# The last 64 features in two token halves: matmuls of 64 weight columns instead of zero-padded ones of 128

## The chip, the cores and the metric

The kernel runs as one program on one core of a Trainium2 chip. The metric is the device time of that core in microseconds (us). Three runs of the kernel before are shown, and one more execution was profiled.

## The reference, cut to what matters

32 images become 38 tokens of 192 features each, in float32. Two layers follow. The first has a state-space scan whose four step inputs come from small networks, and a mixture of eight feed-forward experts of which each token uses two. The second has a mamba block that is run in both directions of the sequence, and a mixture of eight 192 by 192 experts:

```python
h = h + _L0_attn_ref(_layernorm(h), ...)   # scan, 16 states per feature
h = h + _L0_ffn_ref(_layernorm(h), ...)    # 2 of 8 experts, 768 wide
h = h + _L1_attn_ref(_layernorm(h), ...)   # down to 96, mamba forward and backward, up to 192
h = h + _L1_ffn_ref(_layernorm(h), ...)    # sum over e of gate[e] * (x @ expert_w[e].T + expert_b[e])
```

In the mamba block `z` and `x` are projections of 96 values to 192, the convolution over four taps and the step width `dt` (24 to 192) give 192 features as well, and `y = (h * C).sum(-1)` sums 16 states for each of the 192 features.

## The kernel before

**Layout.** Features lie on partitions, tokens along the free axis. The images are worked on in four groups of eight, T = 304 tokens a group. 192 features don't fit on 128 partitions, so each result has a main part, features 0 to 127 for 304 tokens, and a rest, features 128 to 191. In the packed layout the rest of tokens 0 to 151 lies on partitions 0 to 63 and that of tokens 152 to 303 on partitions 64 to 127, in 152 further columns (T to PK = 456). VectorE, ScalarE and GpSimd so handle 456 columns of 128 partitions.

**How the rest is computed before.** Every matmul of the kernel has weights of more than 64 columns, most of exactly 128. For a packed rest two of them accumulate into the same 128 partitions: the first with the rest's 64 weight columns followed by 64 columns of zeros, on the first token half, the second with 64 zero columns followed by the weights, on the second half. The weights lie in memory as main, zeros, rest, zeros (with_blanks, line 2222), and halves (line 159) cuts the three windows of 128 columns out of it. This is done for the z projection (project_z), the four convolution taps (project_taps), the step width (packed), delta (to_delta) and, with a matrix of ones (gsumr), for the sum over states (add_states). A float32 matmul shows in the trace as two weight loads and two matmul instructions.

The expert mixture's rest isn't packed. mixture_rest (line 2042) multiplies 304 tokens by 128 weight columns, of which only the first 64 results are used: 12 products (GX holds eight gated inputs for features 0 to 127 and four for the rest, two experts in each) and one for the biases. Or, its output, has 64 partitions of 304 columns.

**Passes.** A first pass over the groups runs the first layer's scan; then come the routed experts of the first layer in 34 blocks of 128 rows, from before the end of the first scan to about 530 us; then a second pass runs the second layer. In the second pass part_a(g) holds the twelve steps (QSTEPS) of the forward scan of group g, part_b(g) those of the backward scan. A step treats two blocks of eight features times 16 states: VectorE forms b times w (line 1293) and scans (line 1304), GpSimd multiplies by C (line 790), TensorE sums the 16 states (sum_step). Steps 0 to 7 are main, 8 to 11 rest. Around the steps the order is written out by hand for each engine, in program order, with semaphores between the engines: at n = 1 to 6 of part_a(g) the mixture of group g - 2 (mixture), at n = 9, 10, 11 its rest in three parts (5, 4 and 4 matmuls), and between them the layer norm's mean, centring and variance, then in part_b(g) at n = 1, 2, 7, 8, 9 the projections of group g + 1. VectorE adds the mixture's rest (add_mixture_rest, line 1551) in part_b at n = 0, before it goes on with the scan's next step; ScalarE has copied the residual into Or at n = 7 of part_a (line 1089).

**Queues.** SyncE issues the loads of the scan's rows (line 510), which are filled into four slots in a ring, and the stores (store, line 608): out_m from Om and out_r from Or, after VectorE's addition. store_end waits for their landing and frees Om and Or.

**The end.** After the last scan, part_a(None, 3, None, 2), part_b(None, 3, None) and part_a(None, None, None, 3) run without one: the mixture of group 2 and the output of group 3, then the router of group 3, its gates by way of memory, its mixture, its rest, the addition and the store.

Nearly all matmuls go through one helper (line 1670), so the rows name their operands: PR or V with CM is a state sum, HB with CM is z or a tap, aP with CM a step width, WX with CM the mixture and its rest, q_LW with CM the mixture's biases (with q_LW as the weights: the transposed logits), q_RS and p_RS a variance.

## Time and profile before

| what | value |
|---|---|
| median of 3 runs | 959.54 us (952.37, 959.54, 961.0) |
| profiled execution | 956.27 us, its span 954.5 us |
| mean granted TensorE clock | 0.893 of full speed |
| TensorE matmuls | busy 740.4 us (78%), 3608 instructions |
| TensorE weight loads | busy 587.9 us (62%), 3608 |
| VectorE | 566.5 us (59%), 968 |
| ScalarE | 404.1 us (42%), 876 |
| GpSimd | 394.6 us (41%), 311 |

The profiled execution is a run of its own; its time less its span is the 1.8 us that lie around the recorded instructions. A matmul's duration runs from its start to a modelled end and overlaps with that of the next, so busy time counts some time twice, and the pace is read from starts. The rows below are of this execution. In an entry such as `128*128 128x152` the first pair is the weights (rows by columns), the second the moving data (partitions by columns).

### The profile page before, as it was taken

To read this page: it belongs to the slowest core of one execution; us is meant where nothing else is said; L and a number is where in the kernel's file an instruction comes from. 1 tells how busy PE (TensorE), PEld (TensorE's weight loads), DVE (VectorE), ACT (ScalarE), POOL (GpSimd) and SP (SyncE) were. 2 spreads that over 40 slices of the span, in tenths; PEclk is the share of its full clock that TensorE was granted. 3 is DMA by queue.
4 is the path that set the end of the run, shared out by engine and by line. 5 is a ranking of instruction groups with operands and counts; after the bars stand their busy time and mean duration, and the time that the engine had idled before them with its cause. 6 is when DMAs were issued, how large, how long until landed. Compare 5 with 4: busy or idle time off the path is not lost. (4 is left out here: it accounts for less than half of the span.)

```text
span 954.5 us, 11504 instructions
## 1 busy us (share of the span) xinstructions
PE 740.4 (78%) x3608; PEld 587.9 (62%) x3608; DVE 566.5 (59%) x968; ACT 404.1 (42%) x876; POOL 394.6 (41%) x311
## 2 busy tenths in 40 slices
PE   7977878586458879997999568777769885986756
PEld 5644656455327869997999356555556664764434
DVE  4167769679766532322112587988777787789320
ACT  1548275374134224332445446373617361733110
POOL 1045745655673311312013344544538333734503
PEclk9899899798678889999999789898979998997977
DMA  9469755355495567798786878697588657866221
GB/s 351 133 208 337 215 152 151 90 134 142 117 273 144 166 182 242 233 281 248 218 244 190 206 194 217 176 224 190 143 229 216 150 156 224 226 165 180 79 72 27
DMA packets 84668, 179.51 MB, mean 188 GB/s; under 512 B 12740, under 2 KB 32832, under 8 KB 83840
## 3 DMA queue, kind: packets, MB, share of 16 engines
q1 hardware_dynamic: 79776, 171.55, 64.1%
q0 software_dynamic: 4832, 7.24, 2.6%
q8 instruction: 28, 0.46, 0.2%
q14 instruction: 32, 0.26, 0.1%
HBM read 158.02 MB, written 20.69 MB: 187 GB/s over the span
## 5 line engine op out<-in xcount | busy, mean ns | idle before, releaser
L1670 PE MATMUL PS<-PR,CM 128*128 128x304 f32 (+1 forms) x672 | 184.1, 415 | 89.4 <-POOL PR L790 60.6
L790 POOL TENSOR_TENSOR PR<-ST,V 128x608 f32<-128x608 f32 x96 | 142.2, 1481 | 185.7 <-DVE ST L1304 160.2
L1670 PEld LDWEIGHTS PS<-PR,CM 128*128 128x128 f32 x672 | 125.7, 219 | 131.6 <-POOL PR L790 74.4
L956 ACT ACTIVATE dA<-dA,negA 128x304 f32<-128x304 f32 x192 | 93.7, 539 | 151.5 <-DMA BB<-rows_d 151.2
L1304 DVE TENSOR_TENSOR_SCAN ST<-dA,PS 128x608 f32<-128x608 f32 x96 | 136.3, 1420 | 15.3 <-ACT dA L956 11.3
L1008 ACT ACTIVATE HID<-PS,WX 128x128 f32<-128x128 f32 x204 | 59.6, 367 | 141.3 <-PE PS L1670 141.2
L703 POOL TENSOR_TENSOR dA<-dA,aP 128x607 f32<-128x607 f32 x48 | 70.7, 1474 | 73.6 <-ACT aP L976 70.8
L1293 DVE TENSOR_TENSOR PS<-BB,PS 128x608 f32<-128x608 f32 x96 | 76.2, 794 | 21.7 <-DMA BB<-rows_d 10.5
L1670 PE MATMUL PS<-XT,WX 128*128 128x128 f32 x408 | 82.5, 285 | 1.0 <-ACT HID L1008 1.0
L1670 PE MATMUL PS<-WX,HID 128*128 128x192 f32 x408 | 76.6, 339 | 8.3 <-DVE XT L1493 8.3
L1670 PE MATMUL PS<-XT,WXR 128*128 128x128 f32 x408 | 81.6, 283 | 0.0
L718 POOL DMA_DIRECT2D outs_d<-xp x34 | 19.2, 564 | 140.8 <-DVE xp L1500 140.7
L1670 PEld LDWEIGHTS PS<-WX,HID 128*128 128x128 f32 x408 | 69.6, 199 | 9.3 <-issue 5.1
L709 POOL TENSOR_TENSOR PR<-PR,ST 128x608 f32<-128x608 f32 x32 | 47.2, 1474 | 58.3 <-DVE ST L1283 58.2
L1283 DVE TENSOR_TENSOR_SCAN ST<-dA,PS 128x608 f32<-128x608 f32 x48 | 67.8, 1412 | 3.2 <-POOL dA L703 1.8
L1500 DVE TENSOR_TENSOR xp<-PS,WXB 128x192 f32<-128x192 f32 x34 | 12.2, 357 | 96.2 <-PE PS L1670 96.2
L1670 PEld LDWEIGHTS PS<-XT,WX 128*128 128x128 f32 x408 | 67.1, 202 | 2.2 <-ACT HID L1008 1.2
L1670 PE MATMUL PS<-WX,CM 128*128 128x304 f32 x192 | 57.0, 438 | 11.7 <-POOL WX L798 11.4
L1670 PEld LDWEIGHTS PS<-XT,WXR 128*128 128x128 f32 x408 | 64.7, 200 | 0.0
L1670 PEld LDWEIGHTS PS<-WX,CM 128*128 128x128 f32 x192 | 37.4, 198 | 27.6 <-POOL WX L798 14.9
L1670 PE MATMUL PS<-HB,CM 96*128 96x152 f32 (+1 forms) x240 | 49.5, 358 | 0.0
L1492 DVE COPY XT<-PS 128x128 f32<-128x128 f32 x34 | 9.8, 289 | 63.5 <-PE PS L1886 52.3
(363 smaller groups left out, 1318.7 us busy)
## 6 DMA issues: line engine op xcount, KB each, us to landing
dA<-rows_d SPq DMA_DIRECT2D x144, 304.0 KB, 4.4
BB<-rows_d SPq DMA_DIRECT2D x144, 304.0 KB, 4.9
WX<-ex_m SPq DMA_DIRECT2D x34, 576.0 KB, 3.9
WX<-ex_m SPq DMA_DIRECT2D x34, 387.0 KB, 3.8
slots_d<-WXR SPq DMA_DIRECT2D x8, 960.0 KB, 8.0
WXR<-ex_r SPq DMA_DIRECT2D x34, 192.0 KB, 4.6
WX<-gates_d SPq DMA_DIRECT2D x4, 1216.0 KB, 6.4
CM<-c SPq DMA_DIRECT2D x1, 4430.0 KB, 19.6
```

Source lines behind the costliest of these rows:

```text
L703: nc.gpsimd.tensor_tensor(now[:, 1:], now[:, 1:], before[:, 0:QB * T - 1], ALU.mult).then_inc(ap_ready.sem, 1)
L709: nc.gpsimd.tensor_tensor(PR3[c % 3], PR3[c % 3], STq[:, c % 2], ALU.mult).then_inc(P.product.sem, 1)
L718: pool.dma_start(outs_d[b // HALF_BLOCKS][at:at + 128, :], YB[:, b % 3, :]).then_inc(out_rows[b % 3], 16)
L790: nc.gpsimd.tensor_tensor(PRq[:, c % 2], STq[:, c % 2], DIRS[k].Cw.unsqueeze(1).broadcast_to([128, QB, T]), ALU.mult).then_inc(q_product.s ...
L956: last = nc.scalar.activation(dAq[:, slot, i, :], dAq[:, slot, i, :], ACT.Exp, scale=negA[:, j:j + 1])
L1008: last = nc.scalar.activation(HX[:, p, f, :], PS[:, wide_bank(b, h), j * 128:(j + 1) * 128], ACT.Gelu, bias=WX[:, p, FFN + f:FFN + f + 1])
L1283: nc.vector.tensor_tensor_scan(flat(STq[:, c % 2], False), flat(dAq[:, slot], False), BP[0], 0.0, ALU.mult, ALU.add).then_inc(P.scanned.se ...
L1293: nc.vector.tensor_tensor(BPq[k], BBq[:, slot], BW[k].unsqueeze(1).broadcast_to([128, QB, T]), ALU.mult).then_inc(b_times_w.sem, 1)
L1304: nc.vector.tensor_tensor_scan(flat(STq[:, c % 2], back), flat(dAq[:, slot], back), BP[k][:, ::-1] if back else BP[k], 0.0, ALU.mult, ALU. ...
L1492: nc.vector.tensor_copy(XT[:, p, 0, :], PS[:, SHARED_BANK, 0:128])
L1500: nc.vector.tensor_tensor(YB[:, p, :], PS[:, SHARED_BANK, 256:256 + D], WXB[:, p, :], ALU.add).then_inc(y_copied.sem, 1)
L1670: return nc.tensor.matmul(out, lhsT, rhs, start=first, stop=last)
```

## The change

The rest is no longer computed with zero-padded weights. The windows of 128 columns are replaced by the 64 weight columns alone (main_rest). The first token half's matmul writes partitions 0 to 63, the second's partitions 64 to 127 of the same columns, and neither adds to the other's. This holds for z, taps, step width, delta and the state sums, with the same number of matmuls as before. The sums' first matmul for the rest in the mamba block, the skip term (SKIP), stays one of 128 columns.

The mixture's rest is packed too: its 13 matmuls of 304 tokens become 26 of 152, each weight being loaded for either half. Or has 128 partitions of 152 columns; ScalarE fills it with two copies instead of one, VectorE's addition covers 128 partitions of 152 columns, and out_r is stored by two transfers instead of one, so that store_end waits for three. The arrays that the host prepares and their zeros stay as they are.

```diff
@@ -156,10 +156,10 @@
-        def halves(name, of=None):
+        def main_rest(name, of=None):
             get = cm if of is None else of
-            return (get(name, 0, 128), get(name, 192, 320), get(name, 128, 256))
+            return (get(name, 0, DM), get(name, DM + DR, DM + 2 * DR))
         ones_tw = sb("ones_tw", [TW, TW])
@@ -226,7 +226,7 @@
         Om = sb("Om", [128, T])
-        Or = sb("Or", [DR, T])
+        Or = sb("Or", [128, HALF])
@@ -329,7 +329,7 @@
         h_loaded, keep_loaded, gathered = sig("h_loaded", 32), sig("keep_loaded", 16), sig("gathered", 16 * 2 * TILES)
-        stored, out_free = sig("stored", 32), sig("out_free", 1)
+        stored, out_free = sig("stored", 48), sig("out_free", 1)
@@ -608,10 +608,12 @@
                 sp.dma_start(out_m[bass.ds(g, 1), :, :].rearrange("g p t -> p (g t)"), Om[:, :]).then_inc(stored.sem, 16)
-                sp.dma_start(out_r[bass.ds(g, 1), :, :].rearrange("g p t -> p (g t)"), Or[:, :]).then_inc(stored.sem, 16)
+                rest = out_r[bass.ds(g, 1), :, :].rearrange("g p t -> p (g t)")
+                sp.dma_start(rest[:, 0:HALF], Or[0:DR, :]).then_inc(stored.sem, 16)
+                sp.dma_start(rest[:, HALF:T], Or[DR:128, :]).then_inc(stored.sem, 16)
             def store_end(g):
-                sp.wait_ge(stored.sem, stored.after(g, 32))
+                sp.wait_ge(stored.sem, stored.after(g, 48))
                 sp.sem_inc(out_free.sem, 1)
@@ -1086,7 +1088,8 @@
                         act.wait_ge(out_free.sem, out_free.after(mix, 1))
-                        nc.scalar.activation(Or[:, :], Q.Hr[:, :], ACT.Copy).then_inc(rest_copied.sem, 1)
+                        nc.scalar.activation(Or[0:DR, :], Q.Hr[:, 0:HALF], ACT.Copy)
+                        nc.scalar.activation(Or[DR:128, :], Q.Hr[:, HALF:T], ACT.Copy).then_inc(rest_copied.sem, 1)
                     if n == 10 and tail is not None:
@@ -1552,7 +1555,7 @@
                 dve.wait_ge(rest_copied.sem, rest_copied.after(g, 1))
-                nc.vector.tensor_tensor(Or[:, :], Or[:, :], PS[0:DR, REST_BANK, 0:T], ALU.add).then_inc(final.sem, 1)
+                nc.vector.tensor_tensor(Or[:, :], Or[:, :], PS[:, REST_BANK, 0:HALF], ALU.add).then_inc(final.sem, 1)
                 dve.wait_ge(final.sem, final.after(g, 1))
@@ -1726,11 +1729,11 @@
-                main, lower, upper = (w[0:BN, :] for w in halves("fb"[k] + "in_z"))
+                main, rest = (w[0:BN, :] for w in main_rest("fb"[k] + "in_z"))
                 out, x = PS[:, Z_BANK, :], hb(0)
                 mm(seqs(out[:, 0:T]), main, x, True, True)
-                mm(seqs(out[:, T:PK]), lower, x[:, 0:IMG // 2, :], True, False)
-                return mm(seqs(out[:, T:PK]), upper, x[:, IMG // 2:, :], False, True)
+                mm(seqs(out[0:DR, T:PK]), rest, x[:, 0:IMG // 2, :], True, True)
+                return mm(seqs(out[DR:128, T:PK]), rest, x[:, IMG // 2:, :], True, True)
@@ -1746,16 +1749,16 @@
                     w, x = tap(s)
-                    mm(seqs(out[:, T:PK]), w[:, 192:320], x[:, 0:IMG // 2, :], s == 0, False)
-                    last = mm(seqs(out[:, T:PK]), w[:, 128:256], x[:, IMG // 2:, :], False, s == 3)
+                    mm(seqs(out[0:DR, T:PK]), w[:, DM + DR:DM + 2 * DR], x[:, 0:IMG // 2, :], s == 0, s == 3)
+                    last = mm(seqs(out[DR:128, T:PK]), w[:, DM + DR:DM + 2 * DR], x[:, IMG // 2:, :], s == 0, s == 3)
                 last.then_inc(in_mm.sem, 1)
...
-                main, lower, upper = (w[0:p, :] for w in halves(name))
+                main, rest = (w[0:p, :] for w in main_rest(name))
                 mm(out[:, 0:T], main, x[:, 0:T], True, True)
-                mm(out[:, T:PK], lower, x[:, 0:HALF], True, False)
-                return mm(out[:, T:PK], upper, x[:, HALF:T], False, True)
+                mm(out[0:DR, T:PK], rest, x[:, 0:HALF], True, True)
+                return mm(out[DR:128, T:PK], rest, x[:, HALF:T], True, True)
@@ -1800,8 +1803,9 @@
                         at = FEAT_BLOCKS - 1 - j
-                        mm(PS[:, bank, T:PK], cm("gsumr", DR + at, DR + at + 128), x[:, 0:HALF], j == MAIN_BLOCKS and not begun, False)
-                        last = mm(PS[:, bank, T:PK], cm("gsumr", at, at + 128), x[:, HALF:T], False, j == FEAT_BLOCKS - 1)
+                        w = cm("gsumr", DR + at, 2 * DR + at)
+                        mm(PS[0:DR, bank, T:PK], w, x[:, 0:HALF], j == MAIN_BLOCKS and not begun, j == FEAT_BLOCKS - 1)
+                        last = mm(PS[DR:128, bank, T:PK], w, x[:, HALF:T], j == MAIN_BLOCKS and not begun, j == FEAT_BLOCKS - 1)
                 return last
@@ -1865,14 +1869,14 @@
                 pe.wait_ge(hid_ready.sem, hid_ready.after(p, 2))
-                (mw, ml, mu), (rw, rl, ru) = halves("d_w2"), halves("d_w2", cr)
+                (mw, mr), (rw, rr) = main_rest("d_w2"), main_rest("d_w2", cr)
                 out = PS[:, MEAN_BANK, :]
...
                 mm(out[:, 0:T], rw, HIDrK[:, :], False, True)
-                mm(out[:, T:PK], ml, HID[:, 9, 0:HALF], True, False)
-                mm(out[:, T:PK], rl, HIDrK[:, 0:HALF], False, False)
-                mm(out[:, T:PK], mu, HID[:, 9, HALF:T], False, False)
-                mm(out[:, T:PK], ru, HIDrK[:, HALF:T], False, True).then_inc(delta_mm.sem, 1)
+                mm(out[0:DR, T:PK], mr, HID[:, 9, 0:HALF], True, False)
+                mm(out[DR:128, T:PK], mr, HID[:, 9, HALF:T], True, False)
+                mm(out[0:DR, T:PK], rr, HIDrK[:, 0:HALF], False, True)
+                mm(out[DR:128, T:PK], rr, HIDrK[:, HALF:T], False, True).then_inc(delta_mm.sem, 1)
@@ -2041,12 +2045,16 @@
+                low, high = PS[0:DR, REST_BANK, 0:HALF], PS[DR:128, REST_BANK, 0:HALF]
                 if part == 0:
-                    mm(PS[:, REST_BANK, 0:T], cm("eb", 128, 256), Q.LWK[:, :], True, False)
+                    mm(low, cm("eb", DM, D), Q.LWK[:, 0:HALF], True, False)
+                    mm(high, cm("eb", DM, D), Q.LWK[:, HALF:T], True, False)
                 each = 2 * MIX_PARTS // REST_PARTS
...
                     name, at = ("ew", i * D) if i < EXPERTS else ("ewp", (i - EXPERTS) * D)
-                    last = mm(PS[:, REST_BANK, 0:T], cm(name, at + 128, at + 256), GX[:, i, :], False, i == 2 * MIX_PARTS - 1)
+                    w = cm(name, at + DM, at + D)
+                    mm(low, w, GX[:, i, 0:HALF], False, i == 2 * MIX_PARTS - 1)
+                    last = mm(high, w, GX[:, i, HALF:T], False, i == 2 * MIX_PARTS - 1)
                 if part == REST_PARTS - 1:
```

## Rows read from the trace of the kernel before

**Rows 1.** The page's chain of waits, shares of the span by engine and line:

```profile
PE PS L1670 12%; DMA BB<-rows_d 7%; DVE ST L1304 5%; DVE PS L1293 3%; ACT dA L956 1%; POOL WX L798 1%; SPq L510 1%; DMA rows_d<-p_WV 0%; SPq L622 0%; DVE q_WV L1360 0%; SPq L621 0%; DVE q_DL L1359 0%; SPq L623 0%; DVE p_TM L1355 0%; DVE q_OM L1357 0%
```

**Rows 2.** Waits of TensorE, whole span: total us, times, longest:

```profile
PE PS L1670 <- POOL PR L790: 60.6, 28, 10.0
```

**Rows 3.** TensorE groups, shapes apart: busy us, mean ns, idle before:

```profile
L1670 PE MATMUL PS<-PR,CM 128*128 128x152 f32 x320 | 57.1, 329 | 19.2 <-POOL PR L790 16.8 <-POOL PR L709 2.3
...
L1670 PE MATMUL PS<-aP,CM 128*128 128x152 f32 x32 | 5.4, 293 | 0.0
...
L1670 PE MATMUL PS<-WX,CM 128*128 128x304 f32 x192 | 57.0, 438 | 11.7 <-POOL WX L798 11.4
...
L1670 PEld LDWEIGHTS PS<-aP,CM 128*128 128x128 f32 x48 | 8.0, 190 | 4.9 <-ACT aP L921 3.0
...
L1670 PEld LDWEIGHTS PS<-p_Hm,CM 128*96 128x96 f32 x4 | 0.7, 163 | 0.3
```

**Rows 4.** Timeline of TensorE, third group's scan: start, us from first start to last end:

```profile
743.78 0.78 PE L1670 MATMUL PS<-q_Hm,ones_d 128*128 128x304 f32 x2 [2.19 <-DVE q_Hr L1562]
744.39 0.68 PE L1670 MATMUL PS<-q_Hr,ones_d 128*128 128x304 f32 x2
...
748.95 0.67 PE L1670 MATMUL PS<-q_LW,CM 128*128 128x304 f32 x2
...
751.50 1.20 PE L1670 MATMUL PS<-PR,CM 128*128 128x152 f32 x8
752.54 0.68 PE L1670 MATMUL PS<-q_RS,ones_d 128*128 128x304 f32 x2
...
753.56 2.21 PE L1670 MATMUL PS<-WX,CM 128*128 128x304 f32 x8
...
756.64 0.67 PE L1670 MATMUL PS<-p_RS,ones_d 128*128 128x304 f32 x2
...
758.69 2.21 PE L1670 MATMUL PS<-WX,CM 128*128 128x304 f32 x8
760.74 1.20 PE L1670 MATMUL PS<-PR,CM 128*128 128x152 f32 x8
...
771.39 0.62 PE L1670 MATMUL PS<-CM,q_LW 128*102 128x8 f32 x6
771.87 2.31 PE L1670 MATMUL PS<-HB,CM 96*128 96x152 f32 x16
```

**Rows 5.** Timeline of ScalarE and VectorE, same stretch:

```profile
751.31 0.44 ACT L862 ACTIVATE q_SQr<-q_Cr 64x304 f32<-64x304 f32 x1
...
758.96 0.47 DVE L1576 TENSOR_TENSOR m_Xm<-PS,p_RS 96x304 f32<-96x304 f32 x1 [4.44 <-ACT p_RS L872]
...
760.94 0.46 DVE L1555 TENSOR_TENSOR Or<-Or,PS 64x304 f32<-64x304 f32 x1 [0.74 <-PE PS L1670]
```

**Rows 6.** Timeline of TensorE, the same place in the fourth group:

```profile
847.02 0.78 PE L1670 MATMUL PS<-q_RS,ones_d 128*128 128x304 f32 x2 [0.47 <-ACT q_SQr L862]
...
848.14 2.21 PE L1670 MATMUL PS<-WX,CM 128*128 128x304 f32 x8
...
853.27 1.20 PE L1670 MATMUL PS<-PR,CM 128*128 128x152 f32 x8
```

**Rows 7.** Timeline of all engines, the end of the span:

```profile
907.27 0.67 PE L1670 MATMUL PS<-q_LW,CM 128*128 128x304 f32 x2
...
909.82 0.68 PE L1670 MATMUL PS<-q_RS,ones_d 128*128 128x304 f32 x2
...
914.94 0.67 PE L1670 MATMUL PS<-q_Xm,CM 128*128 128x304 f32 x2
...
944.40 0.68 PE L1670 MATMUL PS<-q_LW,CM 128*128 128x304 f32 x2
...
951.26 0.46 DVE L1555 TENSOR_TENSOR Or<-Or,PS 64x304 f32<-64x304 f32 x1 [6.18 <-PE PS L1670]
...
952.13 0.51 SPq L611 DMA_DIRECT2D out_r<-Or  x1
```

## The prediction

> **What bounds the kernel now.** I read the page's chain of waits first, then the groups of instructions with shapes kept apart, then the timeline of the second pass and its end. The chain names TensorE's helper line as its largest share, though the scans of VectorE and the row transfers together have as much [rows 1]: no engine bounds the whole, so a saving on TensorE counts only in the stretches where others wait for it. During most scan steps it is TensorE that waits, for GpSimd's products [rows 2]. What the change touches are 608 matmul instructions of 152 columns (384 in the state sums, of which [rows 3] has 320, 160 in the taps and z, the rest in the step widths and delta) and 104 of 304 columns in the mixture's rest (half of the 192 in [rows 3], and 8 for the bias). A logical fp32 matmul is two instructions with a weight load before each.
>
> Next, the timeline gives the pace. Eight instructions of 152 columns start at 751.50 and their follower at 752.54: 0.130 us each, weight loads hidden. The block from 758.69 to 760.74 holds eight of 304 columns, 0.256 us each [rows 4]. Last, I looked for the places where VectorE stands still for this work. In the third group's scan it waits until 760.94 for the mixture's rest [rows 5], in the fourth the matmuls run on from 848.14 to 853.27 with the same consumer [rows 6], and at the end two runs of mixture's rest stand on the path, from 907.27 to 914.94 and from 944.40 to 951.26, the second with nothing beside it but VectorE waiting 6.18 us [rows 7].
>
> **Prices.** Call p the pace of one new instruction of 152 columns into 64 partitions, and s the cost of going from 128-column matmuls to 64-column ones or back. No row shows either.
>
> p: the two halves of a pair write different partitions from different token halves. If they run beside each other, two take the time of one: 0.130/2 = 0.065 us. If they don't, p is 0.130. Also something must issue and load: six short matmuls with 102-column loads go from 771.39 to 771.87, 0.080 us each [rows 4], an upper end for the load and issue of a shorter one. I take 0.072, between 0.065 and 0.080. A fall below 0.065 is excluded, for each half still streams all its columns. The upper end: a load of 128 columns takes 190 ns, one of 96 163 [rows 3], so 64 columns take some 54 ns of loading; if that is not hidden, p is 0.130 + 0.054 = 0.184.
>
> s: the kernel before never changes the width of the array in use, so I bound it. The lower end is 0, if a change is free. For a full stop, the tail of a matmul is its duration less its pace, 0.293 [rows 3] less 0.130 = 0.163 us, and the first pair after an idle stretch takes 744.39 - 743.78 = 0.61 us where a running pair takes 0.51 [rows 4], 0.10 more. Together 0.27; with a whole load of 0.19 in the open it is 0.36. I take 0.27, because these two parts are durations of this trace, while nothing in it speaks for a free change. Beside that stands the Trainium skill, "TensorEngine Tiling (Array Packing)", section "Tiling Modes": a change of mode drains TensorE, while tiles of one mode run independently. By that the sum stays as below; with free changes it would be about 7 us better.
>
> **The sum, part by part.**
>
> Mixture's rest: 13 logical matmuls of 304 columns become 26 of 152, so 26 instructions become 52 a group. With overlap that is 52 x 0.072 = 3.74 us for 26 x 0.256 = 6.66.
> - Third group: three blocks, with two state sums joined to them, 748.95 to 752.54, 753.56 to 756.64, 758.69 to 760.74 [rows 4], 8.72 us. After: 68 x 0.072 + 5 x 0.27 = 6.25, or 2.5 less. ScalarE's squares are only there at 751.75 [rows 5], which takes 0.3 of it, and VectorE has its three scalings of 0.47 to do after 758.96, so it is late next: I count -2.0.
> - Fourth group: the variance waits for the squares already [rows 6], so the first block gains nothing. From 848.14 on, 5.13 us become 40 x 0.072 + 0.27 = 3.15: -2.0.
> - The next to last mixture: 20 instructions and two changes replace 907.27 to 909.82, 32 and two replace the 4.10 before 914.94: 1.98 + 2.84 for 2.56 + 4.10, -1.8.
> - The last: 3.74 + 0.27 for 6.66, -2.65.
>
> Store: at the end the third transfer is issued after the other two, +0.51 us [rows 7]; in the earlier groups it lies beside fills that run four slots ahead, and costs at most 0.51 each if that lead is gone. Copy: two ScalarE copies for one, next to its waits for landings; at most another 0.45 us a group. The last addition is 152 columns for 304, a gain under 0.2 us that I leave out.
>
> Everything else: a block of eight (a state sum or delta) goes from 1.04 to 8 x 0.072 + 0.54 = 1.12, four instructions (z, step widths) from 0.52 to 0.83, sixteen taps from 2.08 to 1.69. Of these about ten, six and two lie in stretches where TensorE is followed by others: 0.8 + 1.9 - 0.8 = +1.9; the rest wait for GpSimd anyway [rows 2]. I take half, +1.0, with 0 and 1.9 as ends.
>
> Sum: -2.0 - 2.0 - 1.8 - 2.65 + 0.5 + 1.0 = **-7.0 us**. The profiled execution took 956.27 us (span 954.5 and 1.8 around it), so it would be 949.3; it lies 3.3 below the median of the runs shown, and on the median the sum gives 952.5, which I predict.
>
> **Rivals.**
> 1. Full overlap and cheap changes (p 0.065, s 0.1). The waits in the four stretches end 2.4, 2.5, 2.9 and 3.2 earlier, less 0.5 for the store, and the other blocks gain some 2.5: -13, or 946.5. For it: the halves share nothing but the bank. Against: six short matmuls need 0.080 each.
> 2. The halves don't run beside each other: slower. Place: every narrow block; price: p stays 0.130, so no block gains and each pays two changes, 0.54. The four stretches cost 1.5 + 0.3 + 1.2 + 0.4, the store 0.5; the other eighteen blocks 9.7, of which I take half: +8.8, or 968; all of it +13.6, 973. It decides from p above about 0.10, where the sum above passes zero. For it: matmuls start strictly in order in this trace, and no row shows two that stream at once. Against: each wants only half of the array's columns.
> 3. The loads come into the open as well (p 0.184): the four stretches cost 5.1 + 2.5 + 4.0 + 3.2, the store 0.5, the other blocks 8.5 to 17: +24 to +32, about 987. Against: loads are hidden in blocks of one width [rows 4]. The Trainium skill, "TensorE: Matmul & The Clock Gate", section "Part 3: Packing small matmuls — row/col tiling", says that a load overlaps matmuls in flight only when the row group differs, and here both halves use all rows; the trace of before contradicts it for full width.
> 4. The gains are given back: VectorE resumes earlier and waits for the row transfers or for ScalarE instead, and only the end keeps its 4 us: with the other blocks -1 to -4, near 957. For it: transfers of rows are the second largest share of the chain [rows 1].
>
> **Chances.** The forecast 0.43, rival 1 0.15, rival 2 0.24, rival 3 0.10, rival 4 0.08. The three runs shown differ by 0.9%, so I take 1%, 9.6 us, as what can be told from no change. Faster by more: most of rival 1 and a quarter of the forecast's spread, 0.13 + 0.13 = 0.26. Slower by more: rival 3 and somewhat over half of rival 2, with a margin for a last case such as a lower granted clock of a TensorE that is less busy, 0.26. The rest is 0.48. The range reaches from below rival 1 to the upper end of rival 2, 942 to 975, and leaves rival 3 out. The forecast's own range is 947 to 957.
>
> **What would show it.** Right: narrow instructions start in steps of near 0.07 us within a block, with gaps of near 0.27 at its borders; the last run of mixture's rest takes about 4 us; VectorE's wait before its addition in the third group's scan shrinks or goes to ScalarE. TensorE's busy time says little, for the overlapped instructions are each counted whole. Wrong: steps of 0.13 or more, borders well over 0.3 us, new waits of VectorE in the first pass, or a lower granted clock in the second.

## The result, and the profile after

The changed kernel takes 949.6 us (median of 13 runs, 942.4 to 956.0), the kernel before 956.0 in 13 runs beside it: a ratio of 0.9922, 95% interval 0.9896 to 0.9948, or 7.5 us less (5 to 10; the two medians alone differ by 6.4). The forecast was 7.0 less. By the bound of 1% set in the prediction this is the case "within 1%". The profiled execution took 950.07 us, span 948.3, against a span of 954.5. Comparisons leave out disturbed runs, those more than 1.5% above the fastest of their kernel; this matters most for E12, where two of six are left out and the profile is of one of them, and for E7, where two of ten are.

The chain of waits and the largest wait of TensorE, to be held against [rows 1, 2], its line now being L1673:

```profile
PE PS L1673 11%; DMA BB<-rows_d 6%; DVE ST L1307 5%; DVE PS L1296 3%; ACT dA L958 1%; SPq L510 1%; DMA rows_d<-p_WV 1%; POOL PR L792 1%; SPq L624 0%; SPq L623 0%; DVE q_WV L1363 0%; DVE q_DL L1362 0%; SPq L625 0%; DVE q_OM L1360 0%; DVE q_gate L1222 0%
```

```profile
PE PS L1673 <- POOL PR L792: 69.4, 28, 10.8
```

TensorE waits 8.8 us more for GpSimd's products: much of what its shorter sums save seems not to have been on the path, which E2 puts to the test. The groups of TensorE's instructions, shapes apart (busy us, mean ns of one, idle before), for [rows 3]:

```profile
L1673 PE MATMUL PS<-PR,CM 128*64 128x152 f32 x320 | 36.8, 364 | 26.7 <-POOL PR L792 24.1 <-POOL PR L711 2.5
...
L1673 PE MATMUL PS<-WX,CM 128*64 128x152 f32 x192 | 14.4, 298 | 0.0
...
L1673 PEld LDWEIGHTS PS<-WX,CM 128*64 128x64 f32 x192 | 12.6, 140 | 1.7 <-issue 1.7
```

Of the mixture's rest 192 narrow instructions are busy 14.4 us together, 0.075 each, though one alone takes 298 ns: they overlap. Timeline of TensorE and then VectorE in the third group's scan (start, us from first start to last end), for [rows 4, 5]:

```profile
751.10 0.48 PE L1673 MATMUL PS<-q_LW,CM 128*64 128x152 f32 x4
751.41 1.20 PE L1673 MATMUL PS<-WX,CM 128*64 128x152 f32 x16
752.45 0.69 PE L1673 MATMUL PS<-PR,CM 128*64 128x152 f32 x8
754.04 0.78 PE L1673 MATMUL PS<-q_RS,ones_d 128*128 128x304 f32 x2 [0.91 <-ACT q_SQr L864]
...
755.26 1.25 PE L1673 MATMUL PS<-WX,CM 128*64 128x152 f32 x16
756.34 0.69 PE L1673 MATMUL PS<-PR,CM 128*64 128x152 f32 x8
756.96 0.78 PE L1673 MATMUL PS<-p_RS,ones_d 128*128 128x304 f32 x2
```

```profile
759.38 0.47 DVE L1579 TENSOR_TENSOR m_Xm<-PS,p_RS 96x304 f32<-96x304 f32 x1 [2.80 <-ACT p_RS L874]
...
760.54 0.30 DVE L1558 TENSOR_TENSOR Or<-Or,PS 128x152 f32<-128x152 f32 x1
```

Sixteen instructions take 752.45 - 751.41 = 1.04 us, 0.065 each; with padded weights eight of the same 152 columns took that time [rows 4]. ScalarE's squares are late next (a wait of 0.91), VectorE's wait for p_RS falls from 4.44 to 2.80, and its addition to Or no longer waits. In the fourth group the addition, at 853.33, is not held up by TensorE: the scaling ahead of it (q_Xr) takes 1.75 us for 0.46. VectorE before and after, then GpSimd after, for [rows 6]:

```profile
850.14 0.46 DVE L1172 TENSOR_TENSOR q_Xr<-q_Cr,q_RS 64x304 f32<-64x304 f32 x1
```

```profile
851.65 1.75 DVE L1175 TENSOR_TENSOR q_Xr<-q_Cr,q_RS 64x304 f32<-64x304 f32 x1
853.33 0.29 DVE L1558 TENSOR_TENSOR Or<-Or,PS 128x152 f32<-128x152 f32 x1
```

```profile
851.52 1.55 POOL L792 TENSOR_TENSOR PR<-ST,V 128x608 f32<-128x608 f32 x1 [2.55 <-PE PS L1673]
```

The same happens in E10 (1.77 us), the only other of the 14 profiles in which this scaling of the fourth group starts while GpSimd's product runs; in the other twelve it takes 0.46. Before, that product started at 851.56, behind the scaling. The end of the span, TensorE, VectorE and the store, for [rows 7]:

```profile
906.26 0.67 PE L1673 MATMUL PS<-q_Hr,ones_d 128*128 128x304 f32 x2
906.86 0.48 PE L1673 MATMUL PS<-q_LW,CM 128*64 128x152 f32 x4
907.17 1.21 PE L1673 MATMUL PS<-WX,CM 128*64 128x152 f32 x16
908.43 0.78 PE L1673 MATMUL PS<-q_RS,ones_d 128*128 128x304 f32 x2
909.04 0.67 PE L1673 MATMUL PS<-q_SQr,ones_d 128*128 128x304 f32 x2
909.65 2.29 PE L1673 MATMUL PS<-WX,CM 128*64 128x152 f32 x32
911.87 0.78 PE L1673 MATMUL PS<-q_Xm,CM 128*128 128x304 f32 x2
...
941.10 0.48 PE L1673 MATMUL PS<-q_LW,CM 128*64 128x152 f32 x4
941.41 3.27 PE L1673 MATMUL PS<-WX,CM 128*64 128x152 f32 x48
```

```profile
944.73 0.31 DVE L1558 TENSOR_TENSOR Or<-Or,PS 128x152 f32<-128x152 f32 x1 [3.05 <-PE PS L1673]
...
946.00 0.60 SPq L613 DMA_DIRECT2D out_r<-Or  x1
```

The last run is 941.10 to 944.73, 3.63 us for 6.86; the one before it 906.86 to 911.87, 5.01 for 7.67. From the end of the last addition to the end of the span it is 948.3 - 945.04 = 3.26 us, before 954.5 - 951.72 = 2.78.

**A ledger by stretch.** The same instruction starts at two times in two kernels; the change of that difference over a stretch is what the stretch gained (-) or lost. Marks, in times of before: VectorE's centring at 747.16 and its products with the gate at 763.60, 811.86 and 856.14, TensorE's mean matmul of q_Hr at 906.75, its logits at 916.72, the last addition at 951.26, the end of the span. Each column is one profiled execution less that of before, in us:

```
to mark     changed   E1     E2     E3     E4     E5     E6     E9    E11    E12
747.16       +2.07  -1.38  -2.59  +5.08  +1.76  +5.91  +4.38  +3.57  -0.98  +1.61
763.60       -2.63  -2.17  -0.34  -1.60  -1.22  -2.73  +0.97  -2.47   0.00  -2.44
811.86       +1.34  +1.30  -0.32  +1.51  +1.54  +2.26  +0.15  +1.63  -0.09  +1.30
856.14       -1.09  +0.79  -0.06  -0.38  -1.23  +0.30  -0.11  -1.68  +0.75  +1.50
906.75       -0.18  -0.14  -0.54  +0.21  -0.08  -0.35  -0.13  -0.22  -0.24  +0.41
916.72       -2.48  -2.48   0.00  -2.47  -1.35  -2.48   0.00  -2.48   0.00  -2.48
951.26       -3.56  -3.55  -0.89  -3.89  -3.14  -3.93  -0.72  -3.84  -0.60  -3.54
end          +0.33  +0.33  -0.06  +0.34  +0.32  +0.32  -0.04  +1.69  +0.46  +0.34
span         -6.20  -7.30  -4.80  -1.20  -3.40  -0.70  +4.50  -3.80  -0.70  -3.30
```

Read it by rows. The first row scatters over 8 us with no order by what was changed: it holds the landings of the first pass and of the experts' tokens, in the changed kernel one wait of TensorE for gathered tokens (xp) of 7.84 us where before it was 4.54. The 13 runs of one kernel differ by as much. The rows to 916.72 and 951.26 hardly scatter: gains of TensorE with nothing else in the way (the second holds the gates' landing too, worth the -0.6 to -0.9 of E2, E6 and E11).

### The profile page after: what moved, and what is told of

Its sections match the earlier page's. It is cut to its first block and busy times, and to the rows that moved or that the text cites. A ratio compares the mean times of both kernels' runs of the same rounds, so it can differ in the third digit from the quotient of the medians.

```text
span 948.3 us, 11720 instructions
## 1 busy us (share of the span) xinstructions
PE 706.7 (75%) x3712; PEld 530.9 (56%) x3712; DVE 564.7 (60%) x968; ACT 404.9 (43%) x880; POOL 394.9 (42%) x311
## 5 line engine op out<-in xcount | busy, mean ns | idle before, releaser
L1673 PE MATMUL PS<-PR,CM 128*128 128x304 f32 (+1 forms) x672 | 165.3, 434 | 99.7 <-POOL PR L792 69.4
L1673 PEld LDWEIGHTS PS<-PR,CM 128*128 128x128 f32 (+1 forms) x672 | 96.8, 195 | 150.9 <-POOL PR L792 86.5
L958 ACT ACTIVATE dA<-dA,negA 128x304 f32<-128x304 f32 x192 | 93.8, 539 | 156.1 <-DMA BB<-rows_d 155.8
L1673 PE MATMUL PS<-XT,WX 128*128 128x128 f32 x408 | 82.5, 285 | 1.0 <-ACT HID L1010 1.0
L1673 PE MATMUL PS<-WX,HID 128*128 128x192 f32 x408 | 76.6, 339 | 8.6 <-DVE XT L1496 8.6
L1673 PE MATMUL PS<-XT,WXR 128*128 128x128 f32 x408 | 81.2, 282 | 0.0
L1673 PEld LDWEIGHTS PS<-WX,HID 128*128 128x128 f32 x408 | 69.6, 199 | 9.6 <-issue 7.4
L1673 PEld LDWEIGHTS PS<-XT,WX 128*128 128x128 f32 x408 | 66.3, 200 | 3.4 <-issue 1.3
L1673 PEld LDWEIGHTS PS<-XT,WXR 128*128 128x128 f32 x408 | 64.4, 199 | 0.0
L1673 PE MATMUL PS<-WX,CM 128*64 128x152 f32 (+1 forms) x288 | 44.5, 350 | 10.8 <-POOL WX L800 10.8
L1673 PE MATMUL PS<-p_Xm,WX 128*128 128x304 f32 x88 | 33.8, 468 | 17.2 <-ACT HID L903 14.3
L1673 PEld LDWEIGHTS PS<-WX,CM 128*64 128x64 f32 (+1 forms) x288 | 32.2, 163 | 21.6 <-POOL WX L800 12.5
```

The costliest lines, as they stand in the source:

```text
L958: last = nc.scalar.activation(dAq[:, slot, i, :], dAq[:, slot, i, :], ACT.Exp, scale=negA[:, j:j + 1])
L1673: return nc.tensor.matmul(out, lhsT, rhs, start=first, stop=last)
```

## The experiments

Each was timed against the kernel before in five rounds (E7 in three), both on the same chip; how an experiment stands to the changed kernel is read from the two ratios. "Packed" means the new form.

**E1, only the mixture's rest and its store packed.** Edit, on the kernel before: mixture_rest, Or, its copies, addition and store from the changed kernel.

```
-                    last = mm(PS[:, REST_BANK, 0:T], cm(name, at + 128, at + 256), GX[:, i, :], ...)
+                    mm(low, w, GX[:, i, 0:HALF], False, ...)
+                    last = mm(high, w, GX[:, i, HALF:T], False, ...)
```

> The kernel before with the mixture's rest, its sum, its copies and its store in the new form, and everything else (state sums, z, taps, step widths, step table) as before. Theory 'only the end counts': the two rest runs at the end of the kernel give all that shows in the total; the run behind the last gating takes 3.6 us instead of 6.9, the one before it 5.0 instead of 7.7, and the time is 6 us under the kernel before, the same as the whole change within 1 us. Theory 'clock': the thinner state sums are what lowers the granted clock between 700 and 900 us (0.93 to 0.83 in 760 to 830 us), so here, where they stay wide, the clock stays at 0.90 or more there, and the time is 2 to 3 us under that of the whole change. Theory 'row transfers': what the third and fourth group gain in their scans goes to later landings of rows whatever the clock does; the time equals that of the whole change and a wait of VectorE or ScalarE for BB rows is longer than before by 1 to 3 us. By the prediction's own terms for the rest it is 8 us under before.

951.1 us, ratio 0.9932 (0.9897 to 0.9967). **E2, only the state sums packed.**

```
-                        mm(PS[:, bank, T:PK], cm("gsumr", DR + at, DR + at + 128), x[:, 0:HALF], ...)
-                        last = mm(PS[:, bank, T:PK], cm("gsumr", at, at + 128), x[:, HALF:T], ...)
+                        w = cm("gsumr", DR + at, 2 * DR + at)
+                        mm(PS[0:DR, bank, T:PK], w, x[:, 0:HALF], ...)
+                        last = mm(PS[DR:128, bank, T:PK], w, x[:, HALF:T], ...)
```

> The kernel before with only the state sums in the new form (64 weight columns per token half). Theory 'only the end counts': no difference from before, within 1 us, since VectorE's scan sets the step (2.35 us) and the block is 0.5 us shorter under its cover. Theory 'clock': the granted clock between 700 and 900 us falls from 0.92 to about 0.85, the chains of TensorE at the ends of stages run at half speed, and the time is 1 to 3 us over before. Theory 'row transfers': no difference from before.

956.3 us, ratio 1.0009 (0.9974 to 1.0044). **E3, the changed kernel without the packed sums** (E2's edit undone).

> The changed kernel with only the state sums put back to 128 zero-padded weight columns. Theory 'only the end counts': the same time as the changed kernel, 6 to 7 us under before. Theory 'clock': the granted clock between 700 and 900 us is back at 0.90 or more and the time is 1 to 3 us under the changed kernel. Theory 'row transfers': as the changed kernel within 1 us, and the waits for BB rows in that stretch as long as there.

950.0 us, ratio 0.9918 (0.9886 to 0.9951). The three agree: the mixture's rest brings the gain, the sums nothing that shows (+0.9 us, -2.5 to +4.2), and what is left of the change (z, taps, steps) nothing that shows between E1 and the changed kernel. The clock theory had the lower clock right; the 1 to 3 us that it asked for don't show, but lie within these intervals. The stretch 760 to 830 us of the kernel before, the changed kernel, E1, E2 and E3 in this order (busy us and count of PE, PEld, DVE, ACT, POOL, then granted clock, DMA share, GB/s):

```profile
760.00:830.00 70.00, 55.13 (x246) 41.70 (x245) 54.56 (x77) 34.51 (x74) 35.44 (x24) 0.93 0.72 192
```

```profile
760.00:830.00 70.00, 53.55 (x246) 35.56 (x243) 54.07 (x78) 35.06 (x74) 35.12 (x24) 0.83 0.74 195
```

```profile
760.00:830.00 70.00, 55.77 (x237) 41.70 (x237) 51.84 (x75) 35.46 (x76) 36.47 (x25) 0.90 0.78 200
```

```profile
760.00:830.00 70.00, 57.09 (x242) 41.93 (x241) 53.45 (x77) 36.32 (x77) 36.98 (x25) 0.85 0.75 205
```

```profile
760.00:830.00 70.00, 53.29 (x253) 37.08 (x252) 50.20 (x74) 33.86 (x71) 32.47 (x22) 0.90 0.78 195
```

With packed sums the granted clock is 0.83 and 0.85, with wide ones 0.90, and 0.93 before. No difference in time shows; that TensorE waits for GpSimd there anyway is the likely reason, not shown by itself. Where TensorE doesn't wait, a low clock can still eat a gain. E1's timeline in the fourth group, for [rows 6], and its granted clock from 847 to 851 us:

```profile
846.82 2.00 PE L1673 MATMUL PS<-WX,CM 128*64 128x152 f32 x16
...
848.75 2.18 PE L1673 MATMUL PS<-PR,CM 128*128 128x152 f32 x8
...
850.86 1.25 PE L1673 MATMUL PS<-WX,CM 128*64 128x152 f32 x16
```

```profile
847.00:849.00 2.00, 2.00 (x17) 1.53 (x16) 0.71 (x2) 1.56 (x4) 0.00 (x0) 0.54 1.02 257
849.00:851.00 2.00, 2.00 (x10) 1.84 (x12) 0.14 (x1) 0.65 (x2) 0.00 (x0) 0.60 1.04 264
```

The sixteen from 846.82 take 1.93 us and the eight after them 2.11, twice the 1.04 that each takes at the full clock: 2 us, what the packing saves there. E1's sums are wide, so packed sums are not what lowers the clock here.

**E4, low halves first, then high ones,** inside each part of the mixture's rest.

```
-                    mm(low, w, GX[:, i, 0:HALF], ...)
-                    last = mm(high, w, GX[:, i, HALF:T], ...)
+                for half, lo in ((low, 0), (high, HALF)):
+                    for i in range(part * each, (part + 1) * each):
+                        ...
+                        last = mm(half, cm(name, at + DM, at + D), GX[:, i, lo:lo + HALF], ...)
```

> The changed kernel with the order inside each part of the mixture's rest turned: first all products of the low token half, then all of the high half, so that two neighbours write the same 64 partitions; same instructions, same weights, same number. Theory 'the halves run side by side' (a low and a high instruction share TensorE's columns at the same time): the pace of one instruction goes from 0.064 to about 0.127 us, the run at the end from 3.6 to about 6.6 us, the one before it from 5.0 to about 7, and the time is 4 to 5 us over the changed kernel, close to before. Rival 'an instruction with 64 columns is half as long by itself': the pace stays at 0.064 us and the time does not change.

952.4 us, ratio 0.9952 (0.9922 to 0.9982). Neither theory holds as written. The run at the end, E4:

```profile
943.44 4.06 PE L1673 MATMUL PS<-WX,CM 128*64 128x152 f32 x48
```

From 943.13 to the addition at 947.54 it is 4.41 us: 0.78 more than 3.63, not 3. Windows of 0.2 us tell why; behind PE stands the number of instructions that touch the window. First the changed kernel, then E4:

```profile
941.80:942.00 0.20, 0.20 (x8) 0.20 (x6) 0.00 (x0) 0.00 (x0) 0.00 (x0) 1.00 0.00 0
```

```profile
943.60:943.80 0.20, 0.20 (x5) 0.20 (x2) 0.11 (x1) 0.00 (x0) 0.00 (x0) 1.00 0.00 0
943.80:944.00 0.20, 0.20 (x5) 0.20 (x4) 0.00 (x0) 0.00 (x0) 0.00 (x0) 1.00 0.00 0
945.00:945.20 0.20, 0.20 (x7) 0.20 (x4) 0.00 (x0) 0.00 (x0) 0.00 (x0) 1.00 0.00 0
947.00:947.20 0.20, 0.20 (x3) 0.20 (x2) 0.00 (x0) 0.00 (x0) 0.00 (x0) 1.00 0.00 0
```

In the changed kernel a low and a high instruction start together every 0.13 us. In E4 the first low ones start alone, 0.13 us apart (943.44, 943.57, 943.70, ...), and so do the last high ones; between them low and high instructions that are not neighbours run beside each other. So one instruction holds its half for 0.13 us, and the halves do run side by side. Some instructions even start out of the order in which they are listed: the fifth low one starts at 943.96 with another beside it, though eight low ones are listed first. The trace doesn't name the half; this is read from the spacing.

**E7, products of zero weights between the pairs** of the last mixture's rest.

```
+                    if g == GROUPS - 1 and i < 2 * MIX_PARTS - 1:
+                        if i < MIX_PARTS:
+                            mm(PS[:, REST_BANK, 0:16], cr("end"), GX[:, i, 0:16], False, False)
+                        else:
+                            mm(PS[0:DR, REST_BANK, 0:16], cm("gsumr", 0, DR), GX[:, i, 0:16], False, False)
```

> The changed kernel with extra products of zero weights, 16 moving columns wide, put between the pairs of the last group's mixture rest (they add nothing to the sum): behind each of the first six pairs one with 128 weight columns, behind each of the next five one with 64 columns into the low partitions. The pairs take 0.13 us per two instructions. If the price of a change between 128 and 64 columns is the prediction's 0.27 us, each of the six gaps with 128 columns adds 2 x 0.27 us and its own two short instructions, some 0.6 us or 3.6 in all, against 0.1 per gap for the others. If it is the 0.10 us that the changed kernel shows where such a run begins, each gap adds some 0.25 us, 1.5 in all. The run at the end takes 7.5 or 5.4 us instead of 3.6, and the time follows it.

954.1 us, ratio 0.9959 (0.9919 to 0.9999); over all ten runs the median is 954.08 / 954.74 = 0.999 of the kernel before. Timeline of TensorE:

```profile
937.05 0.48 PE L1673 MATMUL PS<-WX,CM 128*64 128x152 f32 x4
937.46 0.40 PE L1673 MATMUL PS<-WX,CR 128*128 128x16 f32 x2
937.79 0.48 PE L1673 MATMUL PS<-WX,CM 128*64 128x152 f32 x4
...
940.73 2.35 PE L1673 MATMUL PS<-WX,CM 128*64 128x152 f32 x34
```

A round with a 128-column product takes 937.79 - 937.05 = 0.74 us, one with a 64-column product 0.375 (pairs in the last group start at 941.04, 941.42, 941.79), a pair alone 0.26. The run takes 7.07 us (936.06 to 943.13), between the 7.5 and the 5.4 that were expected. If the two products cost the same but for the width, two changes of width cost 0.74 - 0.375 = 0.36, 0.18 each. At the borders in the changed kernel it is less or slightly more: the entry at 906.86 comes 0.60 after two instructions of 0.256, 0.09 more; the exit at 908.43 comes 1.26 after sixteen of 0.065 start, 0.22 more.

**E5, E6, E8, E12: where the row buffers lie.** In the profiles of the packed kernels the rows land later than in the others and their transfers hold the engines longer. A narrower Or moves all tiles behind it, so I moved them again: by an unused tile of 32 bytes (E5: behind Or; E8: ahead of WXR, a tile of expert weights; E6: E5's tile, in the kernel before), or back to where they were, by the old width (E12).

```
E5, E6  +        spare = sb("spare", [128, 8])
E12     -        Or = sb("Or", [128, HALF])
        +        Or = sb("Or", [128, T])[:, 0:HALF]
```

> The changed kernel with an unused tile of 32 bytes per partition declared behind Or. In the changed kernel Or is half as wide (608 bytes per partition instead of 1216), so every tile declared after it lies 608 bytes lower, the two buffers into which the rows land (dA, BB) among them: from 185728 and 195456 bytes, multiples of 64, to 185120 and 194848, 32 over a multiple. The spare tile puts them at 185152 and 194880, multiples of 64 again. Theory 'place': rows land later in a buffer that lies 32 bytes off; here the first landing of the fourth group's second scan half comes 9.6 us after the issue of its first read, as in the kernels with the old place (9.7 and 9.5), instead of 11.0, the reads' share of the 16 engines is 64.1% instead of 65.7, ScalarE's waits for BB rows sum to 151 us instead of 156, and the time is 2 to 4 us under that of the changed kernel. Rival 'schedule': the landings are later because the transfers meet others at other times; nothing of this moves, and the time equals that of the changed kernel within 1 us.

> The kernel before, untouched but for an unused tile of 32 bytes per partition behind Or, which moves the row buffers dA and BB from a multiple of 64 bytes to 32 over one. Theory 'place': the first landing of the fourth group's second scan half comes 11.0 us after its first read instead of 9.7, the reads' share of the 16 engines is 65.7% instead of 64.1, and the time is 2 to 4 us over the kernel before. Rival 'schedule': no difference.

> The changed kernel with the unused tile of 32 bytes declared ahead of WXR instead of behind Or: it moves the row buffers to multiples of 64 bytes, as the kernel before has them, and besides the buffers into which expert weights (WXR, WXB), patches and gathered tokens (xp) land, which lay 32 over such a multiple in both kernels. Theory 'place': 2 to 4 us under the changed kernel by the rows, and up to 2 us more where a stage waits for those other transfers (TensorE's waits for xp are 14 us in the kernel before). Rival 'schedule': the time equals that of the changed kernel.

> The changed kernel with Or declared at its old width (1216 bytes per partition) and only the first 608 bytes used, so that every buffer lies at exactly the address it has in the kernel before. Theory 'place', in any form in which an address matters: the rows of the fourth group's second scan half land 9.5 to 10 us after their first read, the reads' share of the 16 engines is 64 to 65%, and the time is 1 to 3 us under the changed kernel. Rival 'meeting' (the transfers of that stretch meet at other times because TensorE's work ahead of them is shorter): the landing stays at 11 us or more, the share at 65.5%, and the time is that of the changed kernel within 1.5 us.

E5 951.1 us, ratio 0.9934 (0.9899 to 0.9969); E6 960.5, 1.0053 (1.0030 to 1.0077); E8 950.2, 0.9952 (0.9913 to 0.9991); E12 946.8, 0.9855 (0.9820 to 0.9889); over all six E12 runs the median is 946.82 / 958.13 = 0.988 of the kernel before. The reads' queue (packets, MB, share of 16 engines) of the kernel before and E6, then of the changed kernel, E5 and E12:

```profile
q1 hardware_dynamic: 79776, 171.55, 64.1%
```

```profile
q1 hardware_dynamic: 79776, 171.55, 64.8%
```

```profile
q1 hardware_dynamic: 80096, 171.55, 65.7%
```

```profile
q1 hardware_dynamic: 80096, 171.55, 65.5%
```

```profile
q1 hardware_dynamic: 80096, 171.55, 64.2%
```

ScalarE's decay of dA and what it waited for, the changed kernel and E12:

```profile
L958 ACT ACTIVATE dA<-dA,negA 128x304 f32<-128x304 f32 x192 | 93.8, 539 | 156.1 <-DMA BB<-rows_d 155.8
```

```profile
L958 ACT ACTIVATE dA<-dA,negA 128x304 f32<-128x304 f32 x192 | 93.6, 538 | 152.1 <-DMA BB<-rows_d 151.7
```

All kernels sort by dA's address: at 185728 (before, E2, E11, E12) the share is 63.9 to 64.2% and the wait 150.5 to 153.6 us; at 185760 (E6) 64.8 and 157.2; at 185120 and 185152 (the others) 65.3 to 65.9 and 155.3 to 158.8. A share is of the span; share times span, the time of the transfers, sorts them more clearly: 610 to 612 us at 185728, 621 in E6, 617 to 627 in the others. The place matters, then, and E6 shows it by itself with 5 us (3 to 7), though its tile moves every tile behind Or and not the rows' buffers alone. But "multiples of 64" was wrong, since 185152 is one, and E5 and E8 gain nothing. Of the four addresses only 185728 is a multiple of 128 bytes, so that rule would fit all 14 profiles; no run tested it, and what makes a place good stays open. The landing named in the expectations does not follow the place: 11.9 us in E5, 9.9 in E6, 11.0 in E12. That the old place makes the packed kernel faster too is likely, not settled: E12's six runs are few.

**E9 and E11: the third store.** After the third group's gain all packed kernels lose 1.3 to 2.3 us by 811.86. The place is the first landing of the fourth group's second scan half. The first read and the start of ScalarE's decay in the changed kernel:

```profile
796.81 0.55 SPq L510 DMA_DIRECT2D dA<-rows_d  x1
...
807.84 0.99 ACT L958 ACTIVATE dA<-dA,negA 128x304 f32<-128x304 f32 x2 [14.93 <-DMA BB<-rows_d]
```

11.03 us; before, 9.71. E9 stores out_r in one transfer, E11 stores it in two in the kernel before; E10 is E9 with E5's tile.

```
E9   -                sp.dma_start(rest[:, 0:HALF], Or[0:DR, :]).then_inc(stored.sem, 16)
     -                sp.dma_start(rest[:, HALF:T], Or[DR:128, :]).then_inc(stored.sem, 16)
     +                sp.dma_start(rest.rearrange("p (h t) -> h p t", h=2), Or[:, :]).then_inc(stored.sem, 16)
```

> The changed kernel with out_r stored by one transfer again instead of two (the same bytes, from 128 partitions of 152, its rows in 608-byte pieces). In the kernels with the packed mixture the rows of the fourth group's second scan half land 11.0 to 11.9 us after their first read, in those without it 9.5 to 9.9; the group's landings ahead of its first store (at 778 us) show no such difference. Theory 'third store': the one transfer more per group shifts all later transfers against each other; here the landing comes after 9.6 us again, and the time is 1 to 2 us under the changed kernel, 0.5 of it at the end of the kernel by the store itself. Rival 'meeting': the landing is later because the gates' and the rows' transfers meet at another time; it stays at 11 us or more, and only the end is 0.3 to 0.5 us shorter.

> The changed kernel with out_r stored by one transfer and with the row buffers put back on multiples of 64 bytes by an unused tile of 32 bytes behind Or. Theories 'third store' and 'place' together: 3 to 5 us under the changed kernel, since moving the buffers off cost the kernel before 5 us (interval 3 to 7). Rival: neither shows in the total; the time is that of the changed kernel within 1.5 us, as it was with the buffers alone put back.

> The kernel before with out_r stored in two transfers, one per token half, from its Or as it is, and nothing else changed. Theory 'third store': the rows of the fourth group's second scan half land 11.0 us after their first read instead of 9.7, and the time is 1 to 2 us over before. Rival 'meeting': the landing stays at 9.5 to 10 us, and the time is that of before within 0.5 us.

E9 951.8 us, 0.9961 (0.9928 to 0.9993); E10 953.3, 0.9967 (0.9933 to 1.0002); E11 956.4, 1.0008 (0.9973 to 1.0044). The landing stays at 11.2 in E9 and 11.3 in E10, and 9.7 in E11; with E12's 11.0 that says: neither the third store nor the place makes it. Nor are E9 and E10 faster than the changed kernel, as the two theories had it: the single store costs 1.4 us more at the end (4.6 for 3.26). Ten kernels with a packed mixture show 11.0 to 11.9, four without 9.5 to 9.9. "Meeting", the rival that is left, was not tested by itself; the cause stays open.

## Why the prediction was right, step by step

The total came out at -7.5 for -7.0, but by terms that were off in both directions; that it came so close is in part luck.

- **p** was forecast at 0.072 us and is 0.065, the lower end: the halves run side by side (E4). Rivals 2 and 3 fall with this; the 64-column loads of 0.140 us, 48 beside the 3.27 us of the last run, stay hidden. The prediction's 54 ns for such a load left out its fixed part; nothing hung on it. The Trainium skill's sentence in "TensorE: Matmul & The Clock Gate", "Part 3: Packing small matmuls — row/col tiling", that a load overlaps matmuls in flight only when the row group differs, is contradicted by this run, where all loads use all rows.
- **s** was forecast at 0.27 and is 0.09 to 0.22 (E7: 0.18). The prediction's two parts together were too much, by a fifth to two thirds. A change of width is not free. The Trainium skill, "TensorEngine Tiling (Array Packing)", "Tiling Modes", says that a change of mode drains TensorE; the trace agrees that it costs something, 0.09 to 0.22 us, and no run shows whether a drain is the reason.
- **The last mixture**, -2.65: measured 3.63 - 6.86 = -3.23, by p and s. **The next to last**, -1.8: -2.47 or -2.48 in nine of ten packed profiles, all but E4. **The store**, +0.5: 3.26 for 2.78, as forecast.
- **The third group**, -2.0: -2.63 here, and the stall goes where the prediction put it, to ScalarE's squares and VectorE's scalings. But the landing behind it takes 1.34 back. That is rival 4's mechanism with half of its price, and the sum had no term for it.
- **The fourth group**, -2.0: this step failed. Between 811.86 and 856.14 the packed profiles show -1.68 to +1.50, the changed kernel -1.09. The sum priced TensorE at the full clock and took it that nothing else came late. ScalarE's squares came 5.1 us after VectorE's centring there instead of 4.5, for it stands behind the landing of rows. From the variance to the addition it is 6.45 us before (847.02 to 853.47) and 4.07 in E9 (850.60 to 854.67), more than the forecast 2.0 less. In the changed kernel it is 4.98 (848.35 to 853.33), for the scaling that runs beside GpSimd's product takes 1.3 us longer; in the five packed profiles with a granted clock of 0.57 to 0.74 in this stretch (E1, E5, E7, E8, E12) it is 5.5 to 7.0.
- **Everything else**, +1.0: the sums alone give +0.9 us (-2.5 to +4.2, E2), and E1 without sums, taps, z and steps has the changed kernel's ratio within 0.1%. Either end of the term, 0 and 1.9, fits. That the blocks lie under GpSimd's products [rows 2] is the likely reason. The +2.07 of this profile ahead of 747 us is scatter of landings.
- **Rival 1** had the prices right (p 0.065, s 0.1) and the time wrong: of its 13 us the two runs at the end give 5.7, the third group 1.3 net, the fourth 1.1 here, and of the rest no gain shows. The lower granted clock, named as a last case, came, and packed sums with it cost nothing that the time shows (E2).

What the prediction did not see is that the new Or moves the row buffers: ScalarE waits 155.8 us for rows, 151.7 with the old place (E12). By all six runs of E12 (0.988 for 0.9922) the total may hold 4 us of this, not settled; the packing alone would then be worth more than the forecast, and the move hid it.

## What to carry to other kernels

Count a saving on an engine only at the places where another one waits for it last, and expect what is saved ahead of a transfer to be partly given back at its landing; what is saved at the very end stays. Ask too what an engine that is done earlier sets off beside the others. Two products that fill only half of the output partitions each are worth packing as a low and a high half side by side, in runs long enough to pay a change of width at both ends. When a tile changes its size, keep the tiles behind it where they were, or the comparison measures two changes.

## What the runs showed of the hardware that was not expected

- Low and high instructions run beside each other also when eight of one half are listed ahead of eight of the other: 0.78 us lost in a run of 48 (E4) where strict order, by the expectation, would have cost 3.
- 32 bytes more ahead of the buffers into which transfers land, and of the tiles behind them, with nothing else changed, cost 0.53% (0.30 to 0.77; E6).
- A scaling of VectorE that starts while GpSimd forms a product takes 1.75 and 1.77 us (changed kernel, E10), in the other twelve profiles 0.46.
- Or's 76 KB leave faster in two transfers of 38 KB: 3.26 us from the last addition to the end, against 950.7 - 946.08 = 4.6 in E9's single one from 128 partitions, and 2.78 for one from 64 partitions with rows twice as long.
- TensorE's granted clock between 760 and 830 us fell from 0.93 to 0.85 where only its sums became shorter (E2), and no loss of time shows: +0.9 us (-2.5 to +4.2).
